# A decoder layer on one Trainium2 core: another order of copies and partial tiles, and a prologue in smaller pieces

## The reference, cut to what matters

```
x = layernorm(x + self_attention(x, w_qkv, b_qkv, w_proj, b_proj))   # 16 heads of 16, causal
x = layernorm(x + cross_attention(x, ctx, w_q, w_k, w_v, w_o))       # 16 heads of 64, 77 keys
x = layernorm(x + ffn(x))                                            # no learned scale or shift

def ffn(x):                          # weights are +1 or -1, chosen by booleans k0, k1, k2
    h = concat([x, -x])              # 512 features
    h = 2 * relu(s0 * (h @ pm(k0)))  # 1024
    h = 2 * relu(s1 * (h @ pm(k1)))  # 1024
    return s2 * (h @ pm(k2))         # 256
```

## Time and profile before

| | |
|---|---|
| median of three runs | 2223.31 us (2220.95 to 2224.39) |
| profiled execution | 2221.23 us |
| its span, from the first to the last instruction | 2219.5 us |
| mean granted TensorE clock | 0.992 |
| TensorE busy | 2122.1 us, 96% of the span |
| VectorE, ScalarE, GpSimd busy | 67%, 51%, 31% |
| chain that ended last, by engine | TensorE 82%, ScalarE 7%, VectorE 5%, issue 3%, DMA 2% |

### The profile page before, as it was taken

The page is one execution under the profiler, slowest core; times in us unless marked ns, Lnnn a source line. Parts: engine busy times, 40 slices in busy tenths (PEclk is TensorE's granted clock), DMA queues, the critical chain, the costliest instruction groups (busy, mean ns, idle before and its releaser), DMA issues.

```text
span 2219.5 us, 54614 instructions
## 1 busy us (share of the span) xinstructions
PE 2122.1 (96%) x18572; PEld 1867.9 (84%) x18572; DVE 1483.1 (67%) x4548; ACT 1128.9 (51%) x2568; POOL 691.3 (31%) x847
## 2 busy tenths in 40 slices
PE   7998789999999999999999999999999999999998
PEld 6888678888888888888888888888888888888887
DVE  5454467677766766776777767666777777677664
ACT  5544455555555554555545555545555455555452
POOL 2000223333333333333333333333333333333331
PEclk9999899999999999999999999999999999999999
DMA  8997532233323333322333233333223332333310
GB/s 258 289 290 216 147 73 64 63 67 72 69 51 75 76 76 76 76 64 63 64 72 74 50 71 76 76 76 76 66 64 62 70 76 50 69 76 76 76 44 10
DMA packets 180580, 196.58 MB, mean 89 GB/s; under 512 B 50130, under 2 KB 135154, under 8 KB 180466
## 3 DMA queue, kind: packets, MB, share of 16 engines
q1 hardware_dynamic: 180532, 195.94, 38.2%
HBM read 69.37 MB, written 58.87 MB: 58 GB/s over the span
## 4 chain that ended last, share of the span: by engine, by line
PE 82%; ACT 7%; DVE 5%; issue 3%; DMA 2%; POOL 1%; SPq 1%; ACTq 0%; POOLq 0%; DVEq 0%
PE ps L1190 13%; PE ps L1372 11%; PE ps L1230 9%; PE ps L1231 9%; PE ps L1338 5%; PE ps L1266 5%; PE ps L1199 4%; PE ps L1213 3%; ACT probs L649 3%; PE ps L1281 3%; PE ps L1255 3%; PE ps L1171 3%; PE ps L1356 3%; PE ps L1140 2%; PE ps L1154 2%
## 5 line engine op out<-in xcount | busy, mean ns | idle before, releaser
L1230 PE MATMUL ps<-r_h,w 128*128 128x256 f16 x2048 | 461.9, 273 | 1.1 <-DVE r_l L838 1.1
L1231 PE MATMUL ps<-r_l,w 128*128 128x256 f16 x2048 | 460.6, 273 | 0.0
L852 DVE CUSTOM_DVE_ANT_0 junk<-ps,causal 128x128 bf16<-128x128 f32 (+1 forms) x1024 | 330.8, 356 | 132.1 <-PE ps L1255 122.0
L498 POOL TENSOR_SCALAR_AFFINE_SELECT probs<-probs 128x512 f32<-128x512 f32 x256 | 163.4, 638 | 471.4 <-ACT probs L649 467.7
L624 ACT ACTIVATE p2r<-ps,low 128x77 f32<-128x77 f32 x1024 | 242.2, 338 | 43.9 <-DVE low L891 43.2
L512 POOL TENSOR_TENSOR p<-p2r,inv 128x308 f32<-128x308 f32 x256 | 200.5, 783 | 198.0 <-DVE inv L902 193.7
L1372 PE MATMUL ps<-vo_h,p2t 128*128 128x256 f32 (+1 forms) x1280 | 239.4, 290 | 8.0 <-DVE p2t L909 8.0
L1230 PEld LDWEIGHTS ps<-r_h,w 128*128 128x128 f16 x2048 | 200.0, 98 | 35.0 <-issue 9.5
L587 ACT ACTIVATE r_h<-ps 128x512 f16<-128x512 f32 x256 | 148.8, 597 | 155.7 <-PE ps L1231 139.6
L522 POOL TENSOR_SCALAR var_eps<-mv 128x2 f32<-128x2 f32 x96 | 21.0, 219 | 655.2 <-DVE mv L827 655.2
L838 DVE SCALAR_TENSOR_TENSOR r_l<-ps,r_h 128x512 f16<-128x512 f32 x256 | 172.4, 684 | 76.5 <-ACT r_h L587 76.5
(11 more groups left out here) (145 smaller groups left out, 4797.1 us busy)
## 6 DMA issues: line engine op xcount, KB each, us to landing
vo_scratch<-vo_out SPq DMA_DIRECT2D x80, 448.0 KB, 4.4
vo<-vo_scratch SPq DMA_DIRECT2D x64, 512.0 KB
q_st<-p2t SPq DMA_DIRECT2D x192, 128.0 KB
k_bd<-p2t SPq DMA_DIRECT2D x192, 128.0 KB, 6.5
q<-q SPq DMA_DIRECT2D x128, 128.0 KB, 2.1
k_bd<-k_scratch SPq DMA_DIRECT2D x64, 154.0 KB, 3.5
x_in<-in_x SPq DMA_DIRECT2D x32, 256.0 KB, 2.7
out<-y SPq DMA_DIRECT2D x32, 256.0 KB, 6.4
```

Of the source, the lines that this page charges most:

```text
L852: dve.tensor_tensor_reduce(out=junk[:, e, b * P:b * P + width], in0=ps[:, bank + b, e * width:(e + 1) * width], in1=causal[:, (1 - b) * P: ...
L1230: pe.matmul(dst, w1[:, kk, m * P:(m + 1) * P], r0_h[:, kk, :], start=kk == 0, stop=False)
L1231: last = pe.matmul(dst, w1[:, kk, m * P:(m + 1) * P], r0_l[:, kk, :], start=False, stop=kk == KF - 1)
```

## The change

Six edits, all of them in the order of the work or in its grain; the arithmetic stays.

- **A.** ScalarE copies the next input (`transposed_x`) ahead of the fourth `self_probs`, instead of behind it.
- **B.** VectorE runs `self_output(i, 1)` ahead of `self_output_low(i, 0)`.
- **C.** The units of the cross probabilities begin with the partial tile, and the third unit's transposes stand ahead of the first output, so that the three outputs of group 0 follow one another (in group 1 a score lies ahead of the last).
- **D.** VectorE adds epsilon; GpSimd only takes the power.
- **E.** In the prologue the split weights come in four chunks behind pairs 4 to 7 of groups 0 and 1, the binary weights one step each behind pairs (2, 4), (2, 5) and (3, 4) to (3, 6), and the scalar coefficients behind (1, 1). The scores of sequence 0 start at (5, 2); two of the eight move into attention 0, to the places that they have in the other passes, and the transposed maximum moves from (5, 5) to (5, 6).
- **F.** At the end the transposes of `x2` stand between the two halves of layer 2 of sequence 30 and use bank 3; layer 0 of sequence 31 has four banks and does not wait for their reading; its layer 2 has banks 6 and 7 and runs six blocks of both halves before the last two.

```diff
-        P2T_UNITS = ((0, 1), (2, 3), (4,))
+        P2T_UNITS = ((4,), (0, 1), (2, 3))
@@ SyncE
-                    if (g, j) == (5, 5):
+                    if (g, j) == (5, 6):
                         stack_max(0, 0)
-                    sp.wait_ge(w_low[3], 1)
+                    sp.wait_ge(w_low[3], 4)
@@ GpSimd
-                pool.wait_ge(d_ag[n], nth(i, 2, 2))
-                pool.sem_inc(passed_pool, 1)
-                pool.tensor_scalar(var_eps[:, n, :], mv[:, n, :, 1], EPS, None, ALU.add).then_inc(g_ve[n], 1)
-                pool.wait_ge(g_ve[n], nth(i, 1, 1))
+                pool.wait_ge(d_ve[n], nth(i, 1, 1))
@@ ScalarE
                 negated_max(i, 1)
+                if more:
+                    transposed_x(i + 1)
                 self_probs(i, 3)
-                if more:
-                    transposed_x(i + 1)
...
+                    if g < 2 and j >= 4:
+                        split_high(g + 3, j - 4)
-                if g < 2:
-                    split_high(g + 3)
@@ VectorE
+                dve.wait_ge(d_ag[n], nth(i, 2, 2))
+                dve.sem_inc(passed_dve, 1)
+                dve.tensor_scalar(var_eps[:, n, :], mv[:, n, :, 1], EPS, None, ALU.add).then_inc(d_ve[n], 1)
...
+                self_output(i, 1)
                 self_output_low(i, 0)
-                self_output(i, 1)
                 self_output_low(i, 1)
...
+                    if g < 2 and j >= 4:
+                        split_low(g + 3, j - 4)
+                    if (g, j) == (1, 1):
+                        coefficients()
+                    if (g, j) in ((2, 4), (2, 5)):
+                        binary_outer(j - 4)
+                    if (g, j) in ((3, 4), (3, 5), (3, 6)):
+                        binary_middle(j - 4)
-                if g == 0:
-                    coefficients()
-                if g < 2:
-                    split_low(g + 3)
-                if g in (2, 3):
-                    binary_weights(g - 2)
@@ TensorE
                 layer1_until(f, 20, 22)
+                cross_transposes(i, 0, 2)
                 cross_output(i, 0, 0)
-                cross_transposes(i, 0, 2)
                 cross_output(i, 0, 1)
                 cross_output(i, 0, 2)
...
                 layer1_until(f, 22, 24)
+                cross_transposes(i, 1, 2)
                 cross_output(i, 1, 0)
-                cross_transposes(i, 1, 2)
                 cross_output(i, 1, 1)
...
-                    if (g, j) == (5, 0):
+                    if (g, j) == (5, 2):
                         pe.wait_ge(const_pool, N_CONST)
                         pe.wait_ge(d_v, 1)
                         pe.wait_ge(q_stacked, 112)
                         pe.wait_ge(k_stacked, 96)
...
-            for b in range(TB):
-                layer2(B - 2, b)
-            pe.wait_ge(d_y3, nth(B - 2, 2, 1))
-            transposed_x2(B - 1)
+            layer2(B - 2, 0)
+            transposed_x2(B - 1, 3)
+            layer2(B - 2, 1)
             pe.wait_ge(d_y3, nth(B - 2, 2, 2))
             for m in range(KF):
-                layer0(B - 1, m)
+                layer0(B - 1, m, LAST_BANKS)
             layer1_until(B - 1, 0, 4 * KF)
-            for b in range(TB):
-                layer2(B - 1, b)
+            for blocks in (range(0, 6), range(6, KF)):
+                for b in range(TB):
+                    layer2(B - 1, b, blocks, 6)
```

More of the change, by code:

```diff
@@ L205, in decoder_layer @@
         passed_dve, passed_pool = sem("passed_dve"), sem("passed_pool")
-        g_ve = [sem(f"g_ve{n}") for n in range(3)]
+        d_ve = [sem(f"d_ve{n}") for n in range(3)]
         g_rs = [sem(f"g_rs{n}") for n in range(3)]
@@ L243, in decoder_layer, with split_chunks @@
         CONTEXT_WEIGHTS = ((wv, wv_h, wv_l), (wk, wk_h, wk_l), (wo, wo_h, wo_l))
-        def split_pieces(job, part):
+        def split_chunks(job, part):
             if job == 3:
-                return qkv_pieces((wqkv_h, wqkv_l)[part]) + [(stage_p, (wp_h, wp_l)[part][:])]
-            return [(stage_q, (wq_h, wq_l)[part][:])]
+                pieces = qkv_pieces((wqkv_h, wqkv_l)[part]) + [(stage_p, (wp_h, wp_l)[part][:])]
+                return pieces[0:1], pieces[1:5], pieces[5:9], pieces[9:]
+            dst = (wq_h, wq_l)[part]
+            return [[(stage_q[:, c // 2, c % 2 * 512:(c % 2 + 1) * 512], dst[:, c // 2, c % 2 * 512:(c % 2 + 1) * 512])]
+                    for c in range(4)]
         SPLIT_SCALE = {3: 1.0, 4: -CROSS_SCALE}
@@ L777, in context_weights_low, with split_low @@
                                   ALU.subtract).then_inc(w_low[n], 1)
[L779 to L781 removed]
+            def split_low(job, c):
+                dve.wait_ge(w_high[job], c + 1)
+                for (src, dst), (_, top) in zip(split_chunks(job, 1)[c], split_chunks(job, 0)[c]):
                     if SPLIT_SCALE[job] == 1.0:
@@ L914, in attention @@
             def attention(i, first, f, g, more=True):
-                if not first:
-                    self_max(i, 6)
-                    self_max(i, 7)
+                self_max(i, 6)
+                self_max(i, 7)
                 if g is not None:
@@ L1045, in coefficients, with binary_outer, binary_middle @@
                 dve.wait_ge(coef, 8)
-            def binary_weights(n):
-                dve.wait_ge(kb_in[n], 16 * (2 - n))
+            def binary_outer(n):
+                dve.wait_ge(kb_in[0], 16 * 2)
                 if n == 0:
                     dve.tensor_tensor(w0[:], kb0[:, 0:KD, :], kb0[:, KD:2 * KD, :], ALU.subtract).then_inc(w_bin, 1)
+                else:
                     dve.tensor_scalar(w2[:], kb2, 2.0, -1.0, ALU.mult, ALU.add).then_inc(w_bin, 1)
-                else:
-                    for c in range(2):
-                        dve.tensor_scalar(w1[:, c * KF // 2:(c + 1) * KF // 2, :], kb1[:, c * KF // 2:(c + 1) * KF // 2, :],
-                                          ffn_coef[:, 1:2], ffn_coef[:, 2:3], ALU.mult, ALU.add).then_inc(w_bin, 1)
+            def binary_middle(n):
+                if n < 2:
+                    dve.wait_ge(kb_in[1], 16)
+                    half = slice(n * KF // 2, (n + 1) * KF // 2)
+                    dve.tensor_scalar(w1[:, half, :], kb1[:, half, :], ffn_coef[:, 1:2], ffn_coef[:, 2:3], ALU.mult, ALU.add)\
+                       .then_inc(w_bin, 1)
+                else:
                     dve.wait_ge(w_bin, 4)
@@ L1201, in tokens_by_weights, with layer0 @@
                 return last
-            def layer0(f, m):
+            def layer0(f, m, banks=(0, 1)):
                 u = m // 2
+                bank = banks[u % len(banks)]
                 if m == 0:
@@ L1208, in layer0 @@
                     pe.wait_ge(d_x2t, nth(f, 1, 1))
-                if m >= 4 and m % 2 == 0:
+                if m >= 4 and m % 2 == 0 and len(banks) == 2:
                     pe.wait_ge(d_r0, nth(f, 4, u - 1))
@@ L1212, in layer0 @@
                     for kk in range(KD):
-                        last = pe.matmul(ps[:, u % 2, (m % 2) * S:(m % 2 + 1) * S], w0[:, kk, m * P:(m + 1) * P],
+                        last = pe.matmul(ps[:, bank, (m % 2) * S:(m % 2 + 1) * S], w0[:, kk, m * P:(m + 1) * P],
                                          x2t[:, kk, :], start=half == 0 and kk == 0, stop=half == 1 and kk == KD - 1)
@@ L1233, in layer1, with layer2 @@
                     last.then_inc(pe_z1, 1)
-            def layer2(f, b, blocks=range(KF)):
+            def layer2(f, b, blocks=range(KF), bank=0):
                 rows = slice(b * P, (b + 1) * P)
@@ L1240, in layer2, with transposed_x2 @@
                         pe.wait_ge(d_r1, nth(f, 4, 3 + kk // 6))
-                    pe.matmul(ps[:, b, 0:D], r1_h[:, kk, rows], w2[:, kk, :], start=kk == 0, stop=False)
-                    last = pe.matmul(ps[:, b, 0:D], r1_l[:, kk, rows], w2[:, kk, :], start=False, stop=kk == KF - 1)
+                    pe.matmul(ps[:, bank + b, 0:D], r1_h[:, kk, rows], w2[:, kk, :], start=kk == 0, stop=False)
+                    last = pe.matmul(ps[:, bank + b, 0:D], r1_l[:, kk, rows], w2[:, kk, :], start=False, stop=kk == KF - 1)
                 if kk == KF - 1:
                     last.then_inc(pe_z2, 1)
-            def transposed_x2(f):
+            def transposed_x2(f, bank=0):
                 pe.wait_ge(d_x2, nth(f, 2, 2))
-                transposes(x2, 0, f, pe_x2t)
+                transposes(x2, bank, f, pe_x2t)
             def scores_by_query(i, n, bank=2):
@@ L1401, in attention @@
                 scores_by_key(i, 1)
-                if f is not None:
-                    scores_by_query(i, 6)
+                scores_by_query(i, 6)
                 filler2(0)
@@ L1406, in attention @@
                 filler2(1)
-                if f is not None:
-                    scores_by_query(i, 7)
+                scores_by_query(i, 7)
                 filler2(2)
```

64 lines of the change are left out of this document (31 added, 33 removed).

## The result

The changed kernel takes 2191.96 us (median of four runs, 2189.37 to 2194.55) against 2223.28 us: a ratio of 0.986, with a 95% interval of 0.9843 to 0.9878. On another chip it took 2189.52 us against 2224.1 us (0.9845, 0.9832 to 0.9859). The forecast was 2189 us, 2177 to 2202. The profiled execution took 2189.37 us with a span of 2187.6 us, 31.9 us less than the span before.

The account below looks back on a forecast made before the run. TensorE, busy 96% of the span, was taken as the bound. Terms 15.9 + 2.7 + 0 + 0.6 + 12.0 + 0 + 3.0 = 34.2 us off 2221.2 gave 2187.0 profiled, plus 2.1: median 2189 us, range 2177 to 2202.

Parts of the forecast that it names:

- A: In the loop, ScalarE's earlier copy of the next input starts the query projection 0.53 us sooner, 30 times: 15.9 us.
- B: In self attention, VectorE's second reciprocal before the first subtraction lets the projection start 0.09 us sooner, 30 times: 2.7 us.
- C: In the cross outputs, partial tile first and outputs in a run: 0 gain, 6 us up or down over 30 attentions.
- D: Epsilon on VectorE: nothing in the loop, 0.15 us each at the end and once in attention 0.
- The pieces: Prologue weights in pieces: three TensorE waits for `v2t_l` and the low clock behind two go, 12.0 us, bounds 6 and 12.
- The scores: Prologue's first scores two pairs later: 0, value outputs waiting for the `vo_out` copy instead; bounds -1 and +8.2 us.
- The end: Last sequence's layers: 3.0 us, of which 2.4 us come from layer 1 starting sooner through the new order and banks.
- the sign of being right: At the end of the run, no wait between the layers of 0.5 us or more except the first.
- the vanishing wait of the scores: Rival: in the prologue the saves land in time and 8.2 us more are won, 2181 us; chance 0.10.
- the outputs that wait more: Rival: in cross attention the two-tile unit comes 0.4 us later, 12 us return, 2201 us; chance 0.13.
- another wait in A's place: Rival: in the loop the delayed exponential or the stacks' transfers cost as much as A wins, 2205 us; chance 0.06.
- the slower case: Rival: two-tile units' copy and subtraction exposed in both cross-attention groups, 2.7 us an iteration, 80 us, 2269 us; chance 0.03.

## Why the prediction was right, step by step

The time lies in the range, 3 us above the forecast, and the main mechanisms were the forecast ones. Several sizes were not, and that the sum came so near is partly luck, as the end of this section shows.

- **A** (15.9 us): right. 0.53 us a pass were forecast, 0.50 came. The exponential's cover, a TensorE that needs the masked values 2 us later, held.
- **B** (2.7 us): the mechanism was right, the size was half. The step that failed is "at a pitch of 0.11, would have let it start at 447.45". The projection can start 0.03 us after the start of the matmul ahead, and 0.17 us a pass came, 5 us in all.
- **C** (0, with 6 us either way): right; 0.03 us a pass the other way. That the wait for `p2t_l` leaves the list, which the prediction did not expect, is no gain, since as much is lost within the outputs; the prediction's sign that it stays near 0.2 us did not come.
- **D** (nothing in the loop): wrong. The step that failed is "in the loop layer-norm waits show nowhere". The view counts idle time from the drawn end of the last matmul, and 0.1 us of waiting lay under it at the transposes of `x1`: 0.105 us a pass, some 3 us in all. Neither wait of B and D is listed, and together they cost 0.28 us a pass, over half of what A gave.
- **The pieces** (12.0 us): the stalls and the low clock behind them went as worked out. The term is too large by the 2.1 us that came back through transfers: the sentence that the queue "does not set the pace on any row of TensorE's there" read the rows of a slower prologue. When TensorE runs ahead by 4 to 9 us and a load stays at its pair of the program, its lead shrinks, and 0.8 us of waiting for the first input became 1.4 to 3.0 in the five profiles. 9.9 us came. With the loads issued earlier the stretch to the first input transposes takes 158.79 us, 12.3 less than the mean of the kernels without the pieces, so the missing part lay with these loads (one profile).
- **The scores** (0): right, and by the mechanism named: the copy of `vo_out` takes over. The Trainium skill (page "DMA: Bandwidth & Descriptors", section "Queues, rings and completion order") says that a DMA engine takes its descriptors in ring order and that a semaphore is written only behind all earlier writes of that engine. The traces agree with it: with one save more ahead of the last six stacks the wait fell from 5.84 to 2.19 us. They do not tell it from engines that are simply busy (DMA share 0.92 behind the wait, 0.95 before). And the queue is only part of the delay: 5.7 us of it are SP's own program, which issues the thirteen stacks before the save.
- **The end** (3.0 us with B and D): right. 2.70 us for the order and the banks, 3.2 us from the last outputs on with C and D. The waits that remain there, after the change, against the earlier trace rows:

```profile
2159.10 0.39 PE L1226 MATMUL ps<-x2t_h,w 128*128 128x256 f16 x2 [0.66 <-DVE y L1028]
...
2161.93 2.48 DVE L843 SCALAR_TENSOR_TENSOR r_l<-ps,r_h 128x512 f16<-128x512 f32 x4
...
2163.87 0.28 PE L1243 MATMUL ps<-r_h,w 128*128 128x256 f16 x1 [1.10 <-DVE r_l L843]
```

Layer 0 waits 0.66 us for `y`, 0.7 us being what was left in the sum, and layer 1 waits until VectorE has done three of its four subtractions (2161.93 + 3 x 0.62 = 2163.8). The sum had that second limit, but the sign of being right, no wait of 0.5 us or more between the layers but the first, did not come: layer 1 waits 1.10 us, more than the 0.54 us before.

By the measured sizes the sum is 9.9 + 21.0 + 1.3 + 3.2 = 35.4 us, the scores and attentions 0 and 1 left out; the medians differ by 31.3 and, on the second chip, by 34.6 us. The forecast had 34.2 us. Its parts missed in both directions, and that they offset each other is luck: the loop gave 0.75 us a pass where 0.62 were forecast (some 3.6 us more over 28 passes), and the prologue 2 us less.

Of the rivals, the vanishing wait of the scores, the outputs that wait more, another wait in A's place and the slower case did not come. TensorE waits for no `v2t_l` behind the pieces, the 2.28 us piece included.

## What to carry to other kernels

A short wait of TensorE hides in the list of waits when the matmul before it is still drawn as running: compare the distance of the starts with the pitch of the same instructions elsewhere, at every place where the operand has only just been written. When a stall is taken out of a stage, ask which transfers are tied to places in the program of that stage; they land as late as before, seen from the clock, and become the next wait. A burst of transfers from one program costs whoever saves through the same engine behind it, first by the time in which they are issued (5.7 us here) and then in the queue, so here a wait for the burst did not go away by moving its reader.

## What the runs showed of the hardware that was not expected

The same part of the program takes different time in different profiles, and the stretches at the lower clock lie differently in it. In attentions 0 and 1, which have no or few fillers, the change should have saved 1.3 us; it took 2.4 us more in the first profile and nothing in the second one of the same kernel (126.18 us from the inputs of sequence 1 to those of 3, where the first had 128.55). Two stretches of 5 us around the begin of attention 1, in the first profile of the changed kernel and in the second (columns as in the earlier trace rows):

```profile
295.00:300.00 5.00, 3.33 (x17) 2.69 (x18) 1.91 (x9) 2.16 (x4) 0.97 (x2) 0.72 0.71 240
300.00:305.00 5.00, 5.00 (x47) 3.86 (x47) 1.57 (x3) 1.04 (x3) 0.30 (x1) 0.60 0.01 4
```

```profile
295.00:300.00 5.00, 3.31 (x21) 2.52 (x19) 2.44 (x16) 1.94 (x4) 1.56 (x3) 0.90 0.83 248
300.00:305.00 5.00, 3.96 (x52) 3.31 (x52) 2.26 (x4) 2.98 (x7) 0.64 (x1) 1.00 0.03 7
```

With nearly the same idle time in the 5 us ahead (3.33 and 3.31 us busy), the clock is 0.60 in the second stretch of the one and 1.00 in that of the other. The clock fell in the second profile too, but earlier, where TensorE stood still for nearly half of the time; in the 5 us before these the first profile had a clock of 1.00:

```profile
290.00:295.00 5.00, 2.71 (x12) 2.43 (x12) 3.20 (x16) 1.30 (x2) 1.07 (x2) 0.76 0.47 119
```

In the first profile the lower clock falls on a stretch in which TensorE is busy throughout (5.00 us). Over all thirteen profiles this part takes 126.10 to 130.67 us, and the kernel before happened to be at the low end in its first profile. Why the clock falls at one place in one run and at another in the next was not settled. It is one reason why a single time of these kernels tells no more than about 3 us, while the length of a pass tells 0.03.
